# The four-bit stage of a fused transformer kernel: VectorE's turn rotated, and h turned by two transfers

## The reference, cut to what matters

```python
def fp4_quant_dequant(x):
    xb = x.reshape(shape[:-1] + (shape[-1] // BLOCK, BLOCK))
    scale = jnp.max(jnp.abs(xb), axis=-1, keepdims=True) / 6.0
    scale = jnp.maximum(scale, jnp.float32(1e-12))
    xn = xb / scale
    idx = jnp.searchsorted(_MID, jnp.abs(xn))
    q = _GRID[idx] * jnp.sign(xn) * scale
    return q.reshape(shape)
...
gate = fp4_linear(x, w_gate)      # 512 -> 1408
y = fp4_linear(x, w_up)           # 512 -> 1408
h = jax.nn.silu(gate) * y
return fp4_linear(h, w_down)      # 1408 -> 512
...
x = x + jnp.tanh(g_ffn[1]) * _L1_ffn_ref(_layernorm(x, axis=-1), ...)
```

## Time and profile before

| | us |
|---|---|
| median of 3 runs | 2104.51 |
| lowest and highest | 2102.99, 2106.59 |
| profiled execution, its own time | 2105.52 |
| its span, first to last instruction | 2103.70 |

### The profile page before, as it was taken

How to read it: one execution, slowest core, us unless ns; L and a number is a source line. 1 busy time by engine, 2 the same in 40 slices (tenths; PEclk the granted TensorE clock), 3 DMA queues, 4 the chain that set the end, 5 groups by cost and what they waited for, 6 DMA issues and landing times. The chain is left out here.

```text
span 2103.7 us, 41058 instructions
## 1 busy us (share of the span) xinstructions
PE 1840.1 (87%) x14583; PEld 1278.3 (61%) x14610; DVE 1431.5 (68%) x2597; ACT 994.1 (47%) x1276; POOL 1243.0 (59%) x1465
## 2 busy tenths in 40 slices
PE   5799999999998459997578999999999977899995
PEld 3467777777776348876346666667667663344442
DVE  4667767867765368886344767768677645899862
ACT  3167767766767497775214434434434341111110
POOL 3267767767766435434212667777677435989962
PEclk9799999999997579999889999999999988999997
DMA  7435445445430321111533444544445553234232
GB/s 207 105 105 130 119 113 130 123 119 131 114 101 25 116 96 36 52 44 35 181 103 88 119 125 134 149 128 136 141 130 148 123 112 78 68 70 93 72 73 56
DMA packets 271258, 222.41 MB, mean 106 GB/s; under 512 B 150008, under 2 KB 239864, under 8 KB 270584
## 3 DMA queue, kind: packets, MB, share of 16 engines
q1 hardware_dynamic: 271096, 220.22, 39.0%
HBM read 129.96 MB, written 67.53 MB: 94 GB/s over the span
## 5 line engine op out<-in xcount | busy, mean ns | idle before, releaser
L739 POOL TENSOR_TENSOR a_p_hl<-a_p,a_p_hl 125x448 bf16<-125x448 f32 x540 | 568.8, 1055 | 437.2 <-ACT a_p_hl L910 408.6
L900 ACT ACTIVATE a_p<-a_psum 125x1344 f32<-125x1344 f32 x192 | 247.8, 1291 | 142.7 <-PE a_psum L1353 132.4
L1084 DVE TENSOR_REDUCE a_nm<-a_psum 112x1 f32<-112x750 f32 x256 | 237.3, 933 | 100.9 <-PE a_psum L1373 100.2
L910 ACT ACTIVATE a_p_hl<-a_p 125x1344 bf16<-125x1344 f32 x192 | 253.9, 1323 | 85.7 <-PE a_psum L1391 82.0
L1391 PEld LDWEIGHTS a_psum<-a_v_st,a_p_hl 125*128 125x128 bf16 x4608 | 177.6, 98 | 46.0 <-issue 26.7
L1391 PE MATMUL a_psum<-a_v_st,a_p_hl 125*128 125x65 bf16 (+2 forms) x4608 | 189.2, 195 | 16.6 <-issue 5.8
L1263 PE MATMUL a_psum<-a_chl,a_w 128*128 128x375 bf16 x768 | 144.0, 334 | 21.5 <-DVE a_w L974 14.7
L1263 PE MATMUL a_psum<-a_chl,kept_w 128*128 128x375 bf16 x768 | 134.7, 327 | 20.6 <-DVE kept_w L974 17.8
L1373 PE MATMUL a_psum<-a_k_st,a_q_st 96*112 96x375 bf16 x512 | 130.8, 342 | 21.7 <-DVE a_nm L1084 15.8
L1263 PE MATMUL a_psum<-a_w,a_chl 128*125 128x512 bf16 x576 | 140.7, 387 | 8.3 <-DVE a_m_parts L1065 5.7
L875 ACT ACTIVATE a_v_st<-a_psum 125x512 bf16<-125x512 f32 x96 | 58.2, 607 | 188.8 <-PE a_psum L1263 188.8
(11 more groups left out here) (263 smaller groups left out, 3892.1 us busy)
## 6 DMA issues: line engine op xcount, KB each, us to landing
a_k<-a_k_tmp SPq DMA_DIRECT2D x64, 375.0 KB, 3.0
a_k_st<-a_k SPq DMA_DIRECT2D x96, 187.5 KB, 3.4
kept_k<-a_k SPq DMA_DIRECT2D x96, 187.5 KB, 3.4
a_c<-in_ctx_t SPq DMA_DIRECT2D x16, 750.0 KB, 5.8
ctx_parts<-a_chl SPq DMA_DIRECT2D x16, 750.0 KB, 9.1
a_chl<-ctx_parts SPq DMA_DIRECT2D x16, 750.0 KB, 6.1
a_q_st<-a_q SPq DMA_DIRECT2D x192, 56.0 KB, 2.2
parts<-a_fhl SPq DMA_DIRECT2D x24, 352.0 KB, 3.7
```

The costliest lines, as they stand in the source:

```text
L739: ins = nc.gpsimd.tensor_tensor(p_hl[0:MC, h % 2, 1, cols], p32[0:MC, h % 2, cols], p_hl[0:MC, h % 2, 0, cols], ALU.subtract)
L900: nc.scalar.activation(p32[0:MC, par, :].rearrange("p (b n) -> p b n", b=3), st[0:MC, :, 0:2 * S], ACT.Exp, scale=scale).then_inc(exp_done, 1)
L910: nc.scalar.activation(p_hl[0:MC, par, 0, :], p32[0:MC, par, :], ACT.Copy).then_inc(phi_done, 1)
L1084: ins = nc.vector.tensor_reduce(out, sm_[0:HALF, 0:2, 0:MK], AX.XY, ALU.max, negate=True)
```

## The change

VectorE's turn is cut at another place: it begins with `make_h` and ends with the moments of tile t+4, `h_divide(t+1)`, `h_powers`, `h_lo(t)` and, last, the residual of tile t-1. The first pass of these steps moves ahead of turn 0, and the loop has four passes instead of five. SP's `turn_hidden(t)` now runs in turn t, behind the loads and ahead of the store, as two transfers of 11 blocks each: the high part when ScalarE has cast it and down(t-1) has ended, the low part when `h_lo(t)` is done. TensorE runs down's 22 products with the high part first, then waits for the low part and runs the other 11.

```diff
             def turn_hidden(t):
 
+                sp.wait_ge(hhi_ready, t + 1)
+                sp.sem_inc(sp_steps, 1)
+                if not (number_known(t) and t == 0):
+
+                    sp.wait_ge(down_ready, t)
+                    sp.sem_inc(sp_steps, 1)
+                sp.dma_start(hqT[:, 0, :, :], hb[:, 0, :], transpose=True).then_inc(hiT_in, 16)
                 sp.wait_ge(hb_ready, t + 2)
                 sp.sem_inc(sp_steps, 1)
-
-                sp.wait_ge(y_ready, t + 1)
-                sp.sem_inc(sp_steps, 1)
-                sp.dma_start(hqT[:, :, :, :].rearrange("p a c s -> p (a c) s"),
-                             hb[:, :, :].rearrange("p a f -> p (a f)"), transpose=True).then_inc(hT_in, 16)
+                sp.dma_start(hqT[:, 1, :, :], hb[:, 1, :], transpose=True).then_inc(loT_in, 16)
...
             def turn(t, par):
-                if in_range(t - 1):
-                    turn_hidden(t - 1)
                 if in_range(t + 2):
                     turn_input(t + 2, par)
...
+                if in_range(t):
+                    turn_hidden(t)
                 if in_range(t - 1):
...
                 if not (number_known(t) and t == 0):
 
-                    act.wait_ge(hT_in, t * 16 + 1)
+                    act.wait_ge(hiT_in, t * 16 + 1)
                 nc.scalar.activation(hb[:, 0, :], hq[:, :], ACT.Copy).then_inc(hhi_ready, 1)
...
             def h_lo(t, par):
                 dve.wait_ge(hhi_ready, t + 1)
+                if not (number_known(t) and t == 0):
+
+                    dve.wait_ge(loT_in, t * 16)
                 nc.vector.tensor_tensor(hb[:, 1, :], hq[:, :], hb[:, 0, :], ALU.subtract).then_inc(hb_ready, 1)
 
             def turn(t, par):
-                if in_range(t + 3):
-                    x_moments(t + 3)
-                if in_range(t):
-                    h_divide(t, par)
-                    h_powers()
-                if in_range(t - 1):
-                    h_lo(t - 1, 1 - par)
                 for g in range(NG):
...
+                if in_range(t + 4):
+                    x_moments(t + 4)
+                if in_range(t + 1):
+                    h_divide(t + 1, 1 - par)
+                    h_powers()
+                if in_range(t):
+                    h_lo(t, par)
                 if in_range(t - 1):
                     dve.wait_ge(xres_in, t * 16)
                     dve.wait_ge(down_ready, t)
...
                 if in_range(t - 1):
-                    pe.wait_ge(hT_in, t * 16 + 1)
+                    pe.wait_ge(hiT_in, t * 16 + 1)
 
                     pe.wait_ge(y_ready, t)
                     for c in range(FC):
-                        for j, (a, b) in enumerate(SPLIT_TERMS):
-                            ins = nc.tensor.matmul(down[:, :], hqT[:, a, c, :], wd[:, b, c, :],
-                                                   start=(c == 0 and j == 0), stop=(c == FC - 1 and j == 2))
+                        for b in range(2):
+                            nc.tensor.matmul(down[:, :], hqT[:, 0, c, :], wd[:, b, c, :],
+                                             start=(c == 0 and b == 0), stop=False)
+                    pe.wait_ge(loT_in, t * 16)
+                    for c in range(FC):
+                        ins = nc.tensor.matmul(down[:, :], hqT[:, 1, c, :], wd[:, 0, c, :],
+                                               start=False, stop=(c == FC - 1))
                     ins.then_inc(down_ready, 1)
```

More of the change, by code:

```diff
@@ L2269, in fp4_ffn @@
         xhi_ready, xb_ready, xT_in = sem("xhi_ready"), sem("xb_ready"), sem("xT_in")
-        hhi_ready, hb_ready, hT_in = sem("hhi_ready"), sem("hb_ready"), sem("hT_in")
+        hhi_ready, hb_ready, hiT_in, loT_in = sem("hhi_ready"), sem("hb_ready"), sem("hiT_in"), sem("loT_in")
         gu_ready, th_ready, h_made = sem("gu_ready"), sem("th_ready"), sem("h_made")
@@ L2315, in turn_hidden @@
             def turn_hidden(t):
+                sp.wait_ge(hhi_ready, t + 1)
[4 more added lines that the diff above has]
+                sp.dma_start(hqT[:, 0, :, :], hb[:, 0, :], transpose=True).then_inc(hiT_in, 16)
                 sp.wait_ge(hb_ready, t + 2)
                 sp.sem_inc(sp_steps, 1)
-                sp.wait_ge(y_ready, t + 1)
-                sp.sem_inc(sp_steps, 1)
-                sp.dma_start(hqT[:, :, :, :].rearrange("p a c s -> p (a c) s"),
-                             hb[:, :, :].rearrange("p a f -> p (a f)"), transpose=True).then_inc(hT_in, 16)
+                sp.dma_start(hqT[:, 1, :, :], hb[:, 1, :], transpose=True).then_inc(loT_in, 16)
             sp.sem_inc(out_sent, 1)
-            sp.sem_inc(hT_in, 1)
+            sp.sem_inc(hiT_in, 1)
             for t in (2, 3):
@@ L2560, in _ @@
             make_h(0, 0, 2)
-            turns(dve.Fori, turn, lambda i: own.enter_loop(i, 2 * FFN1_LINKS),
-                  lambda: own.leave_loop((T - 4) // 2))
+            x_moments(3)
+            h_divide(0, 0)
+            h_powers()
+            turn(0, 0)
+            with dve.Fori(0, (T - 6) // 2) as i:
+                own.enter_loop(i, 2 * FFN1_LINKS)
+                for n in range(2):
+                    turn(i * 2 + (1 + n), 1 - n)
+            own.leave_loop((T - 6) // 2)
+            for t in range(T - 5, T + 1):
+                turn(t, t % 2)
         @block.tensor
```

## The result

The changed kernel took 2080.02 us (median; 2070.21 to 2085.26) against 2103.75 us before in the same comparison; the ratio is 0.9882, with an interval of 0.9846 to 0.9919. The forecast was 2081.0 (2075 to 2090). Its profiled execution took 2078.63 us, with a span of 2076.8 us.

A forecast was written before the change was run, and what follows sets the result against it. A ring of waits from residual through divide, powers, h_lo and transfer to down was taken to bound the turn, no engine being full. Savings of 7.12, 8.37 and 8.57 us, 24.06 off 2105.52, gave 2081.0 us, range 2075 to 2090.

The forecast's parts named there:

- H(0) to H(1): First turn of fp4_ffn; H(t) marks GpSimd going from h_round(t) to x_round; 21.61 us, claimed unchanged.
- nine steady turns: H(1) to H(10): each turn falls from 22.40 to 21.61 us as the wait for down goes; 7.12 us saved.
- last three turns: H(10) to H(13): h_divide no longer stands behind down; 8.37 us saved.
- H(13) to the start of down(13): Tail: the high half leaves without waiting for h_lo(13), so down(13) starts after 5.29 us, not 13.86; 8.57 us saved.
- start of down(13) to the end: Tail: TensorE still idles some 8 us before, so down stays at 9.53 us and the stretch at 12.87 us.
- if VectorE waits for `x_root`: Sign in the profile after the change that would show the forecast wrong; no size given.
- Part 3: TensorE runs down's high terms first: steady, hides part of the low half's landing; pays in the tail.
- the ring over down: Steady turn: residual, 6.4 us divide and powers, 1.62 h_lo, 5.3 transfer, 7.07 down, each waiting for the one before.
- Nothing on VectorE waits for it: Steady turns: down(t) ends 15.1 us after H(t), its residual stands 30 us after; transfer has 10 us or more cover.
- the rival of a slow one: Half transfer takes 5.3 us like the whole, delaying down(13) and its last products: 2083 to 2085 us; chance 0.08.
- The steady turn did shorten: Answers the rival that steady turns stay at 22.40 us and only the tail's 16.94 is won: 2088.6; chance 0.15.
- VectorE and GpSimd do not take turns: Answers the slower rival: narrow VectorE instructions hold up h_round by 3.74 us, turn 25.35, time 2115; chance 0.03.

The follow-up runs named there:

- the extra instruction: One more 128x512 GpSimd instruction at the head of each x_round, added to the changed kernel: turn 23.00 us, stage 348.85; added to the kernel before: 23.02, 362.85.
- the split alone: Changed kernel with VectorE's turn and loop put back as before, keeping the two transfers and down's high products first: stage 332.21 us, turn 21.63, ratio 0.989.
- the joined kernel: Changed kernel plus residual ahead of moments in turns 0 to 10, last two h_round on VectorE, two down banks, unused products in gaps: stage 323.08 us, ratio 0.9859.
- the rotation only: Changed kernel with one transfer of both halves behind h_lo and down's products in their old order: stage 338.65 us, turn 21.75, ratio 0.9914.
- the old order of products: Changed kernel with VectorE's turn as before, two transfers kept, all 33 down products behind the low half in their old order: stage 341.97 us, turn 21.71.
- Two banks: Changed kernel with two PSUM banks for the down product, so down(t) needs not wait for tile t-1's residual: stage 332.22 us, turn 21.75.
- last `h_round` on VectorE: Changed kernel with h_round of the last two tiles on VectorE instead of GpSimd, residual ahead of them in turns 11 and 12: stage 328.93 us.

## Why the prediction was right, point by point

Stage against stage, the forecast's sum was -24.06 us and the profile gives -22.04. That the median of the run times, 2080.02, lies within 1 us of the forecast is partly luck: the stage gained 2 us less than the sum said, and the scatter ahead of it is larger than either.

| step | forecast | measured |
|---|---|---|
| H(0) to H(1) | no change | +0.04 |
| nine steady turns | -7.12 (21.61 each) | -5.80 (21.76 each) |
| last three turns | -8.37 | -8.24 |
| H(13) to the start of down(13) | -8.57 | -8.65 |
| start of down(13) to the end | 0 | +0.61 |

**The steady turn** was read from the one turn of before in which GpSimd never idled, and the mechanism held: `h_divide` starts right behind H(t) each turn, GpSimd has no wait ahead of `h_round`, and the extra instruction shows that it is the bound. The size was off by 0.15 a turn. "I cost it at nothing", I wrote of the residual's 0.75 us. The cover was there (`x_normalise` waits 0.36 now where rows 1 had 0.90), but the residual's place costs 0.12 of the 0.15 all the same: the split alone and the joined kernel, with the residual ahead of the moments, have 21.63. By the rows it is that `x_lo` meets `x_root` at another instruction, 0.11. The gap hid the time and not the position. One sign that the prediction gave for being wrong, "if VectorE waits for `x_root`", did come (3.2 us in nine turns); it was badly chosen, since the model turn of rows 1 has that wait too, and longer.

**What brought it** I had wrong. The prediction gave the steady gain to the rotation and to the split only what lies in the tail. Split only shows that the two transfers bring the steady gain without any rotation, and the rotation only brings it too; together they give no more, and the rotation on top of the split costs 1.5 us. The step that failed is "Part 3 ... Steady: hides part of the low half's landing": I worked out the split's effect with the rotation already in place, where the ring over down was open. By itself it takes 1.7 us of transfer and 4.7 of products out of a ring that was only 0.8 us too long; the transfer's share alone, with the old order of products, brought 21.71.

**A wait that I left out.** "Nothing on VectorE waits for it" was right, but TensorE waits for VectorE: down(t) needs the bank that the residual of tile t-1 frees, and that residual now comes later. It is TensorE's 5.9 us in ten turns, up to 2.0 at a time, and 7.36 before down(12). Two banks showed that the steady turn doesn't feel it.

**The tail** was right in its main terms. The half transfer takes 3.5 where the line gave 3.57, and the rival of a slow one is out. The last stretch, "as slow as now", was 0.6 us short: the 8 us of idle time ahead of down(13) that the prediction counted on were 5.54, since down(12) had waited for the residual, and still the same 33 products spent longer at the lower clock. What sets that stays open.

**The rivals.** The steady turn did shorten. VectorE and GpSimd do not take turns beyond what rows 1 had: the turn is 21.76 and not 25.35, since `h_round`'s six instructions take 7.60 beside `x_normalise` and `x_scale` in the turn shown. The rule that the prediction cites from the Trainium skill, "SBUF — State Buffer", section "Who interferes with whom", by which whoever comes first fully blocks the other, does not describe this turn. The page leaves `tensor_reduce` out of such blocking, 0.69 us of the 3.74 that were priced; an estimate by the page is then a turn of 24.7, which did not come either. No wait for x inputs on TensorE appeared.

## What to carry to other kernels

A ring of waits can be cut at more than one link, and in this kernel the gains did not add: once it is shorter than the fullest engine's turn, a further cut brought nothing and cost 1.5 us; try each alone. Then look at the last turns for themselves, where in the end no engine is full (TensorE 10.06 of 17.8 us from H(12) to H(13) in the changed kernel): in this kernel they held 16 of 22 us, and 9.5 of the 10.65 us that the joined kernel won over the change. Where one part of a program scatters more than the gain, compare the stage that was edited.

## What the runs showed of the hardware

- **VectorE and GpSimd hold each other up unevenly.** One-column GpSimd instructions that meet a wide VectorE instruction last about as long as it, or longer (0.69 beside `x_lo`; 2.46 in the earlier trace rows, where the divide's product of 1.63 and the first power of 0.89 ran; 0.19 and 0.55 elsewhere). GpSimd's 1.27 us instructions kept their length beside VectorE's narrow ones, and those grew, 0.43 to 1.17 for L2172; beside the 1.62 us of `h_lo` GpSimd's six took 8.26 to 8.92 instead of 7.6. So idle time on one of the two is not free room for work: 0.96 us of it took in 0.73.
- **The clock after a pause.** 22 products took 4.92 us when TensorE had been fed up to 2.13 us before (granted clock 0.98 in that window), 6.39 after an idle 3.71 us (last `h_round` on VectorE), 7.70 after 5.54, and 6.54 in two banks after 8.55:

```profile
2064.35 6.54 PE L2607 MATMUL f_down<-kept_w,f_hqT 128*128 128x512 bf16 x22 [8.55 <-DMA f_hqT<-f_hb]
```

  So a longer pause was not always dearer. Nor was it cheaper: 32 products, 7.07 us at clock 1.00, took 10.12 after 12.33 idle. What decides how many products run slow is open; filling the gap with unused products avoided it.
- **Transposing transfers between SBUF tiles**: 8 blocks of 128 x 128 in 3.1 us, 11 in 3.5, 22 in 5.3. An estimate from these three: a fixed 1.8 to 1.9 us and 0.155 a block. The sum of two halves is 1.7 us more than a whole, but the first is there 1.8 us sooner, and at the end the second was issued 1.6 us behind the first (2059.69 and 2061.27), so part of the two overlaps.
- **Scatter.** The same 1737 to 1752 us of program ahead of the stage differ by up to 15 us from profile to profile; the stage of 334 us differed by 0.1 in two profiles of one kernel.
